# Sixteen-head attention: scores from 32-row tiles of four heads, the mask as a two-row product, softmax read straight from four PSUM banks; 16-bit one-hots in the sorting steps

## The reference

```python
q = (x @ q_w + q_b).reshape(b, n, h, d)
kv = (context @ kv_w + kv_b).reshape(b, s, 2, h, d)
k = kv[:, :, 0]
v = kv[:, :, 1]
attn = jnp.einsum('bnhd,bshd->bhns', q, k) * scale
attn = jnp.where(context_mask[:, None, None, :], -jnp.inf, attn)
attn = jax.nn.softmax(attn, axis=-1)
out = jnp.einsum('bhns,bshd->bnhd', attn, v).reshape(b, n, c)
return out @ proj_w + proj_b
```

## Time and profile before

| | |
|---|---|
| median of 3 runs | 2061.74 us (2060.15 to 2063.43) |
| profiled execution, its own time | 2059.06 us |
| its span in the profile | 2057.4 us |
| PE busy | 1362.1 us (66%) |
| DVE busy | 1012.2 us (49%) |
| POOL busy | 939.7 us (46%) |
| ACT busy | 590.3 us (29%) |
| PE clock granted, mean | 0.827 of full speed |

### The profile page before, as it was taken

How to read it: one execution, slowest core, us unless ns; L and a number is a source line. 1 busy time by engine, 2 the same in 40 slices (tenths; PEclk the granted TensorE clock), 3 DMA queues, 4 the chain that set the end, 5 groups by cost and what they waited for, 6 DMA issues and landing times. The chain is left out here.

```text
span 2057.4 us, 33737 instructions
## 1 busy us (share of the span) xinstructions
PE 1362.1 (66%) x9313; PEld 1130.8 (55%) x9315; DVE 1012.2 (49%) x2562; ACT 590.3 (29%) x1122; POOL 939.7 (46%) x935
## 2 busy tenths in 40 slices
PE   4465837566661368871647589992799997748881
PEld 1365726456660367771444355551599995337771
DVE  3243132455447643336457844333488885363334
ACT  3014511111112045541224122221233333325550
POOL 4116724333321267771105368875455552057771
PEclk9557965788886579995779889996899999869996
DMA  3013125111110411113003135542000000221114
GB/s 91 7 51 103 51 62 84 33 36 32 34 31 0 133 34 51 51 48 94 1 1 85 43 85 105 105 84 59 11 0 0 0 0 6 72 78 52 51 51 137
DMA packets 132016, 105.67 MB, mean 51 GB/s; under 512 B 25577, under 2 KB 114153, under 8 KB 131817
## 3 DMA queue, kind: packets, MB, share of 16 engines
q1 hardware_dynamic: 98368, 64.49, 11.7%
q0 software_dynamic: 23040, 33.06, 7.1%
q10 hardware_dynamic: 10544, 7.34, 1.2%
HBM read 75.22 MB, written 29.62 MB: 51 GB/s over the span
## 5 line engine op out<-in xcount | busy, mean ns | idle before, releaser
L685 PE MATMUL bank<-f_xsT,f_w1e 128*128 128x128 f32 x1472 | 212.4, 289 | 51.2 <-issue 28.0
L685 PEld LDWEIGHTS bank<-f_xsT,f_w1e 128*128 128x128 f32 x1472 | 184.1, 196 | 75.9 <-issue 42.8
L652 POOL DMA_INDIRECT f_xs<-d_xn,f_src x184 | 178.2, 969 | 74.3 <-issue 53.3
L656 POOL DMA_INDIRECT d_y<-f_y,f_dst x184 | 181.5, 986 | 64.1 <-issue 52.4
L693 PE MATMUL bank<-f_w,f_hT 128*128 x1472 | 202.7, 281 | 0.0
L764 DVE TENSOR_TENSOR f_hpre<-bank,f_b 128x512 f32<-128x512 f32 x144 | 99.6, 692 | 195.5 <-PE bank L685 103.7
L199 POOL TENSOR_SCALAR xn<-x,ln_mv,ln_rstd 128x128 f32<-128x128 f32 x56 | 47.3, 854 | 303.3 <-DVE ln_rstd L177 303.3
L693 PEld LDWEIGHTS bank<-f_w,f_hT 128*128 128x128 f32 x1472 | 178.2, 191 | 5.9 <-issue 0.2
L208 PE MATMUL bank<-ident,xn 128*128 128x128 f32 x256 | 48.1, 365 | 186.6 <-DVE xn L186 186.4
L719 ACT COPY f_w1e<-f_w 128x512 f32 x184 | 113.6, 618 | 116.8 <-PEq L1253 77.4
L208 PEld LDWEIGHTS bank<-ident,xn 128*128 128x128 f32 x256 | 41.0, 190 | 193.0 <-ACT xn L222 187.7
(11 more groups left out here) (419 smaller groups left out, 2903.6 us busy)
## 6 DMA issues: line engine op xcount, KB each, us to landing
a_mb<-d_m SPq DMA_DIRECT2D x128, 64.0 KB, 2.5
d_xn<-xn SPq DMA_DIRECT2D x3, 2048.0 KB, 9.6
f_yback<-d_y SPq DMA_DIRECT2D x10, 512.0 KB, 5.3
f_yback<-d_y ACTq DMA_DIRECT2D x10, 512.0 KB, 6.1
f_w<-in_L_ffn_W SPq DMA_DIRECT2D x2, 2048.0 KB, 15.8
a_v<-in_ctx SPq DMA_DIRECT2D x4, 1024.0 KB, 11.3
f_wg<-in_WgT SPq DMA_DIRECT2D x16, 256.0 KB, 2.8
f_wu<-in_WuT SPq DMA_DIRECT2D x16, 256.0 KB, 3.1
```

The source lines that it names most:

```text
L652: nc.gpsimd.indirect_dma_start(xs[:, u % RX, :], None, k.d_xn, bass.IndirectOffsetOnAxis(m.src[:, n:n + 1], 0)).then_inc(gathered[u % RX], 16)
L656: nc.gpsimd.indirect_dma_start(k.d_y, bass.IndirectOffsetOnAxis(m.dst[:, n:n + 1], 0), y[:, u % RT, :], None).then_inc(scattered[u % RT], 16)
L685: last = nc.tensor.matmul(BH[u % 2][:, s * P:(s + 1) * P], w1e[:, u % RT, s * P:(s + 1) * P], xsT[:, u % 2, :], start=True, stop=True)
```

## The change

The eight PSUM banks become slices of one tensor, so that an instruction can read across four of them. Attention becomes one block and works on a pair at a time instead of a sequence:

- All loads are issued at once, and the values, queries and keys are projected in one interleaved list of 8 chunks (16 + 1 + 1 matmuls each). The mask is loaded on two partitions only and scaled to a 16-bit table of 2 rows.
- POOL writes per pair a copy of the queries (`qr`, 128 columns), and the keys four times (`km`, 512 columns), where copy i keeps the i-th head of each group of 32 rows. It adds the output bias to x tile by tile (128 columns).
- PE `scores` are, per pair, 4 matmuls of two rows (16-bit, 256 columns) that start each bank with the mask, and 8 matmuls of 32 rows and 64 weight columns (32-bit, 256 moving columns). Four row groups go to four banks and two sequences to two halves of the partitions. There is one set of four banks.
- DVE reads the 1024 scores of a row from the four banks: one maximum and one subtraction. The scale has moved into the queries' projection, and the mask into the matmuls.
- `weigh` is 8 matmuls with 36 moving columns instead of 2 x 4 with 128; `project_out` is one matmul instead of four; `divide` has 2 + 2 instructions per pair instead of 4 + 4.

In `route`, `ii`, `ri`, the iotas and the token numbers are 16-bit, and all arrays have the 8 tile columns innermost. POOL makes three tables at the start of the block; the product with the token numbers is now DVE's.

```diff
-        ri, ii = tb("ri", [P, 2, NT]), tb("ii", [P, 2, NT])
+        ri, ii = tb("ri", [P, 2, NT], BF16), tb("ii", [P, 2, NT], BF16)
...
+                dve.wait_ge(tables, 3)
                 for g in range(NG):
                     js = slice(g * GR, (g + 1) * GR)
-                    TT(picked[:, js, :], bc(k.iota[:, 0:m.cols], (P, GR, m.cols), 1), bc(fii[:, js], (P, GR, m.cols), 2),
-                       ALU.is_equal).then_inc(tile_hot, 1)
                     wait(dve, one_used, g - 1)
-                    TT(ohr[:, g % 2], bc(k.iota[:], (P, GR, P), 1), bc(fri[:, js], (P, GR, P), 2), ALU.is_equal).then_inc(oh, 1)
+                    TT(picked[:, g % 2], col_of[:], bc(fii[:, js], (P, m.cols, GR), 1), ALU.is_equal).then_inc(tile_hot, 1)
+                    TT(ohr[:, g % 2], row_of[:], bc(fri[:, js], (P, P, GR), 1), ALU.is_equal).then_inc(tile_hot, 1)
+                    dve.wait_ge(tile_hot, 2 * g + 2)
+                    TT(ohi[:, g % 2], picked[:, g % 2], bc(tokv[:, js], (P, m.cols, GR), 1), ALU.mult).then_inc(oh, 1)
...
+                def scores(m, u):
+                    pe.wait_ge(kq_ready, m + 1)
+                    wait(pe, shifted, m)
+                    for g in range(NB):
+                        nc.tensor.matmul(k.bank[g][:, 0:NS * S], row[:],
+                                         drop[:, bass.ds(m, 1), :].broadcast_to((2, NS, S)), start=True, stop=False)
+                    for b in range(2):
+                        for g in range(NB):
+                            rows = slice(32 * g, 32 * (g + 1))
+                            last = nc.tensor.matmul(k.bank[g][b * S:(b + 1) * S, 0:NS * S], qr[u][rows, b * S:(b + 1) * S],
+                                                    km[u][rows, b].rearrange("d h s -> d (h s)"), start=False, stop=True)
                     last.then_inc(s_done, 1)
...
+                def body(m, u):
+                    if not is_last(m):
+                        scores(m + 1, 1 - u)
+                    if not early(m, 2):
+                        turn_heads(m - 2, u)
+                    if not early(m, 1):
+                        weigh(m - 1, 1 - u)
+                    if not early(m, 2):
+                        project_out(m - 2, u)
+                    turn(m, u)
...
+                def shift(m, u):
+                    dve.wait_ge(s_done, m + 1)
+                    nc.vector.tensor_reduce(mx[u][:], found, AX.X, ALU.max).then_inc(maxed, 1)
+                    dve.wait_ge(maxed, m + 1)
+                    wait(dve, turned, 2 * m - 2)
+                    TT(z[u][:].rearrange("r (g h) s -> r g h s", g=NB), found, bc(mx[u][:], (P, NB, NS, S), 3), ALU.subtract).then_inc(shifted, 1)
...
+                def body(m, u):
+                    if not is_last(m):
+                        shift(m + 1, 1 - u)
+                    if not early(m, 2):
+                        add(m - 2)
+                    if not early(m, 1):
+                        divide(m - 1, 1 - u)
+                    if not early(m, 2):
+                        measure(m - 2)
```

More of the change, by code:

```diff
@@ new lines, in multi_head_attention, with early @@
+        PV, OT = k.bank[6], k.bank[7]
+        found = k.psum[:, 0:NB * CH].rearrange("r (g f) -> r g f", g=NB)[:, :, 0:NS * S].rearrange("r g (h s) -> r g h s", s=S)
+        def pairs(eng, body):
+            for m in range(4):
+                body(m, m % 2)
+            with eng.Fori(2, NT // 2 - 1) as i:
+                body(2 * i, 0)
+                body(2 * i + 1, 1)
+            body(NT - 2, 0)
+            body(NT - 1, 1)
+        def early(m, n):
+            return isinstance(m, int) and m < n
@@ L1676, in _ @@
+                for m in range(4):
+                    body(m, m % 2)
+                pool.wait_ge(q_out, NC)
+                pool.wait_ge(k_out, NC)
+                with pool.Fori(2, NT // 2) as i:
+                    body(2 * i, 0)
+                    body(2 * i + 1, 1)
             @block.tensor
             def _(pe):
[L1679 to L1687 removed]
@@ L1721, in body @@
[L1721 to L1734 removed]
+                pe.wait_ge(wl, 144)
@@ new lines, in turn @@
+                def turn(m, u):
+                    pe.wait_ge(expd, m + 1)
+                    for q in range(2):
+                        wait(pe, pT_ready, 2 * m - 1 + q)
+                        for c in range(4):
+                            last = nc.tensor.transpose(k.bank[4 + q][:, c * P:(c + 1) * P],
+                                                       z[u][:, 8 * q + 2 * c:8 * q + 2 * c + 2, :].rearrange("r h s -> r (h s)"), k.ident[:])
+                        last.then_inc(turned, 1)
@@ new lines, in weigh, with turn_heads @@
+                def weigh(m, u):
+                    pe.wait_ge(pT_ready, 2 * m + 2)
+                    wait(pe, o_ready, m)
+                    for c in range(NC8):
+                        last = nc.tensor.matmul(PV[:, c * 2 * VW:(c + 1) * 2 * VW], pT[u][:, c, :],
+                                                vb[:, bass.ds(2 * m, 2), c, :], start=True, stop=True)
+                    last.then_inc(pv, 1)
+                def turn_heads(m, u):
+                    pe.wait_ge(o_ready, m + 1)
+                    wait(pe, added, m)
+                    nc.tensor.transpose(OT[:, 0:P], o[u][:].rearrange("r c h d -> r (c h d)"), k.ident[:]).then_inc(o_turned, 1)
@@ new lines, in exp, with copy_turned @@
+                def exp(m, u):
+                    act.wait_ge(shifted, m + 1)
+                    nc.scalar.activation(z[u][:], z[u][:], ACT.Exp).then_inc(expd, 1)
+                def copy_turned(m, u):
+                    for q in range(2):
+                        act.wait_ge(turned, 2 * m + q + 1)
+                        if q == 0:
+                            wait(act, pv, m - 1)
+                        nc.scalar.copy(flat(pT[u][:, 4 * q:4 * q + 4, :]), k.bank[4 + q][:]).then_inc(pT_ready, 1)
@@ L1772, in _ @@
+                copy_heads(NT - 1, 1)
             @block.vector
             def _(dve):
[L1774 to L1787 removed]
```

395 lines of the change are left out of this document (166 added, 229 removed).

## The result

The changed kernel takes 2031.12 us (median of 4 runs, 2030.65 to 2032.36), the kernel before beside it 2060.94: a ratio of 0.9857 (95% interval 0.984 to 0.9874). It is faster, by 30 us (1.4%), where 1948 us and 113 us less were forecast, and it lies outside the range (1922 to 1988). The profiled execution took 2030.91 us, its span is 2028.7, and the mean granted clock fell from 0.827 to 0.774.

A forecast was written before the change was run, and what follows sets the result against it. The attention loop was taken as bound by PE, the sorting by DVE. From 2059.1 us, minus 76.7 (loop), 16.4 (front) and 21 (sorting), came 1945; the median lying 2.7 higher gave 1948 us, range 1922 to 1988.

The forecast's parts named there:

- The clock: Attention loop: rival that PE's clock stays at 1.2 GHz, a pair takes 10 us, the kernel 2106 us; chance 0.03.
- PE's sum at full clock: Attention loop: PE's steps per pair add to 5.03, taken as 5.0 us, with 4.5 and 5.6 as ends.
- switch of tile shape: Attention loop on PE: three switches per pair at 0.17 us each, together 0.5 us.
- the row of the router: Attention scores: four column-group matmuls took 1.00 us in the old trace, so eight score matmuls were put at 0.85 us.
- the rival of no overlap: Attention scores: only column halves overlap, 1980 us, chance 0.12; or nothing overlaps, 2028 us, chance 0.06.
- The loop's length: Attention loop: 4.2 start, 30 periods of 5.0, 14.2 tail; 168.4 against 245.1 us, 76.7 saved.
- DVE and the ring: Attention loop: DVE at 4.1 us a pair and the score-bank cycle at 4.4, both under PE's 5.0.
- the slope: DVE in the attention loop: 1.04 ns per element, giving 1.22 us for a maximum over 1024 elements.
- The ring of the one bank set: Attention loop: scores with mask and switches 1.6, shift 2.5, hand-overs 0.3; 4.4 us a pair.
- The front: Serial start of the attention stage: scores begin near 1464 instead of 1480.5, 16.4 us saved.
- The sorting: Stages 2, 4 and 8: faster 16-bit one-hots and the step behind them, together 21 us saved.
- The rival of an element per cycle: Sorting: 16-bit one-hots still take an element per cycle, so sorting saves nothing; 1969 us, chance 0.07.

The follow-up runs named there:

- the best version: Changed kernel with the mask multiplied into the values on POOL and 108 moving columns in the weighing; 1913.84 us, ratio 0.9293 to the kernel before.
- e1: Kernel before with only the new sorting (`route`); 2182.54 us, ratio 0.985 to the kernel before.
- e5: Changed kernel run again without alteration; 2173.45 us, ratio 0.9866 to the kernel before.
- e8: Changed kernel with 72 moving columns per weighing matmul, the same 36 twice; 2066.25 us, ratio 0.9384 to the kernel before.
- e7: Kernel before with 36 instead of 128 moving columns in the loop's weighing matmuls; 2210.15 us in a single run.

## Why the prediction was wrong

- **The clock** is the step that failed. The rival named it, with the mixture of transposes and short tiles as its reason, and gave it 0.03 on three arguments: that PE has no idle time in the sum, that PE kept its durations behind the router's 32-column tiles, and that the old loop has nine transposes in 65 records at 1.00. The first was true (PE busy 199.16 of 200 us) and excluded nothing. The second was one short passage next to full products. The third was of a loop with 32 full score records a pair, and exactly these the change removes. The runs showed in its place a clock of 0.50 for all but a few us of the loop, and that it is the clock that costs the time: with 126 rows of zeros added to the mask's products, and nothing else changed in the loop, it is 1.00 and stage 7 is 199.0 us long instead of 311.4. What in the mixture of products decides, beyond rows and moving columns, stays open. The price of that rival was too high: 8.0 us a pair instead of 10, 2031 us instead of 2106. With a full clock the forecast would have been too slow: the ratio of the padded kernel, 0.9357, gives 1928 us beside 2060.94 (an estimate), 20 below 1948.
- **PE's sum at full clock** was 5.0 us a pair; the run with padded mask rows shows 4.29 with the same number of instructions and columns. Scores 0.62 instead of 0.85, and no switch of tile shape costs 0.17: the weighing behind the heads and the scores behind the mask start without an idle gap. Transposes (0.87 against 0.88) and weighing (1.70 to 1.82 against 1.90) were right, mask 0.53 against 0.45. The Trainium skill's page "TensorE: Matmul & The Clock Gate" (Part 3) would have had, as an estimate, the scores at about 0.47 and the pair at 4.6, nearer than the row of the router; the trace has 0.62. Row groups run side by side, so both forms of the rival of no overlap fall.
- **The loop's length** was to be 168.4 us. It is 261.8 (from 1444.28 to 1706.10), and 152.1 with the padded mask (1530.44 to 1682.50). This one term is wrong by 93 us, and the result by 83.
- **DVE and the ring.** The maximum and the subtraction take 1.22 us each, as forecast from the slope. In the best version DVE works 0.944 x 4.20 = 4.0 us a pair, against 4.1 in my sum. At half clock none of it matters (PE is busy 199.16 of 200 us); at full clock and without the mask's products a pair takes 4.20 with DVE busy 94% and PE 97%, so the two hold each other. The ring of the one bank set, forecast at 4.4, can't be longer than these 4.20.
- **The front**: 15.6 saved, forecast 16.4.
- **The sorting**: 3.5 + 10.9 + 9.2 = 23.6 saved in its stages, forecast 21; e1 has the same ratio with the sorting alone. The one-hots have the durations of the earlier trace rows: 0.69 for 1024, 0.46 for 576. The rest is overlap: a group of stage 4 takes 1.47 from start to start, where the durations were added to 1.61, since two of its three steps start 0.08 before the record of the one before them ends. The rival of an element per cycle falls.
- **Elsewhere** 5.8 us went in stages 1, 3, 5 and 6. None of my terms had them, and they stay open: the kernel before varies by 5.8 us itself (2057.64 to 2063.43). They may belong to the sorting: of the profiles of e5 to e8, taken beside each other, the three with the new sorting have 913.7 to 915.9 us in these stages, and e7, with the old one, 922.5. No run isolates it.

The sum of these: 93.4 lost in the loop, 0.8 in the front, 2.6 and 5.8 gained elsewhere, 85.8 in all; from the forecast of 1945 for a profiled execution that gives 2030.8, measured 2030.91. That it fits to 0.1 us is partly chance: 0.4 us between the layer norm and the loads, and 0.5 around the span, are in no term and cancel.

## What to carry to other kernels

A busy PE is not a PE at full clock: when a change replaces full products by products of few rows or few moving columns, the granted clock of the new loop belongs into the forecast as a case with real weight, and into the reading of the result as the first view. Where that clock is half, work that costs nothing (zero rows in a small product, repeated columns that leave the weighing's time as it is) can be worth as much as work removed: 112 us of stage 7 for the rows of zeros here, 119 for leaving the products out. And a PE-bound loop at half clock hides its next bound; its steps should be priced at both clocks.

## What the runs showed that I had not expected

- Two rows or 128 in a 16-bit product of 256 columns take the same time (0.52 and 0.53 us for four), and decide between a clock of 0.50 and of 1.00 in a loop of 47 records.
- The granted clock can settle at 0.50 under a PE that is busy 100% of the time, from the first pairs to the last (but for some 3 us at the beginning in one of them), three times in three profiles of the changed kernel. It can also go to and fro in a steady loop (0.74 in windows of 20 us with plain transposes).
- At half clock the weighing (16 records of 128 rows with 36 columns) took 3.28 us against 1.82 at full clock; the records of its weights' loading have a mean of 337 ns against 193 (in the run with padded rows), so that loading follows the clock too.
- Eight 32-row products with 64 weight columns, four row groups by two halves, take 0.62 us from start to start at full clock and 1.09 at half.
